# A three-layer graph convolution kernel: first edges gathered by an accumulating DMA, a new order in conv 2, and conv 1's bias written into PSUM by ScalarE

## What is computed

```python
def gcn_conv(x, W, b, src, dst, n):
    xw = x @ W
    s, d = concat([src, arange(n)]), concat([dst, arange(n)])
    deg = segment_sum(ones_like(d), d); dinv = rsqrt(deg)
    return segment_sum((dinv[s] * dinv[d])[:, None] * xw[s], d) + b

h = relu(layernorm(x))
a = gelu(layer_norm(gcn_conv(h, W1, b1), gamma1, beta1))          # conv 1
a = layer_norm(gcn_conv(a, W2, b2), gamma2, beta2)                # conv 2
x = x + gelu(a + h)
out = x + gcn_conv(relu(layernorm(x)), W3, b3)                    # conv 3
```

## Time and profile before

| what | value |
|---|---|
| median of 3 runs | 3601.41 us (3600.72 to 3601.57) |
| the profiled execution, its own time | 3601.81 us |
| its span, first to last instruction | 3599.8 us |
| busy over the span | PE 85%, DVE 87%, POOL 58%, ACT 46% |
| mean granted TensorE clock | 0.991 |
| data moved | 914.70 MB, 254 GB/s on average |

### The profile page before, as it was taken

One profiled execution on the slowest core, in us unless ns is written; L12 is line 12 of the kernel. 1 busy time (PEld: TensorE's weight loads), 2 busy tenths in 40 slices (PEclk: granted clock), 3 DMA queues, 4 the chain that ended last, 5 costly groups with the idle time before them and its releaser, 6 DMA issues. The chain is left out here.

```text
span 3599.8 us, 61879 instructions
## 1 busy us (share of the span) xinstructions
PE 3057.2 (85%) x16897; PEld 2498.2 (69%) x16897; DVE 3139.7 (87%) x6745; ACT 1650.5 (46%) x2375; POOL 2095.7 (58%) x1853
## 2 busy tenths in 40 slices
PE   8133299999999997999999999999488888888888
PEld 2022188888888886777777777778477777777777
DVE  9899789999999996888888888888688888888887
ACT  0366445555555553777777777777311111111111
POOL 0122256556556654677777777777466666666665
PEclk9999999999999998999999999999799999999999
DMA  3499967777777775888888888888477777777775
GB/s 118 163 408 418 365 215 221 220 225 222 218 223 223 220 219 171 289 295 299 297 296 295 296 298 295 297 295 288 162 241 246 241 246 242 241 246 238 246 240 190
DMA packets 277302, 914.70 MB, mean 254 GB/s; under 512 B 47617, under 2 KB 49511, under 8 KB 277246
## 3 DMA queue, kind: packets, MB, share of 16 engines
q1 hardware_dynamic: 191614, 683.15, 53.1%
q0 software_dynamic: 85632, 230.90, 22.9%
HBM read 653.47 MB, written 308.59 MB: 267 GB/s over the span
## 5 line engine op out<-in xcount | busy, mean ns | idle before, releaser
L840 POOL DMA_INDIRECT g<-H,idx x1062 | 1212.3, 1142 | 614.8 <-issue 428.9
L895 ACT ACTIVATE ahi<-agg 128x1024 fp32r<-128x1024 f32 x354 | 360.9, 1019 | 1039.1 <-PE agg L1171 1039.1
L1189 PE MATMUL out<-Whi,ahi 128*128 128x512 f32 x2832 | 768.9, 393 | 0.0
L1189 PE MATMUL out<-Wlo,ahi 128*128 128x512 f32 x2832 | 763.6, 391 | 0.0
L1189 PE MATMUL out<-Whi,alo 128*128 128x512 f32 x2832 | 761.2, 391 | 0.5 <-DVE alo L1006 0.5
L1162 PE MATMUL agg<-ident,self 128*128 128x128 f32 x2832 | 474.5, 279 | 220.9 <-DVE self L998 171.9
L1189 PEld LDWEIGHTS out<-Wlo,ahi 128*128 128x128 f32 x2832 | 531.6, 188 | 119.6
L1189 PEld LDWEIGHTS out<-Whi,alo 128*128 128x128 f32 x2832 | 531.6, 188 | 114.1 <-DVE alo L1006 1.0
L1189 PEld LDWEIGHTS out<-Whi,ahi 128*128 128x128 f32 x2832 | 510.4, 189 | 91.1
L1162 PEld LDWEIGHTS agg<-ident,self 128*128 128x128 f32 x2832 | 339.3, 142 | 315.8 <-DVE self L998 220.6
L1171 PE MATMUL agg<-sv,vhi 128*128 128x256 f32 x1416 | 384.0, 304 | 66.2 <-DVE sv L986 66.2
(11 more groups left out here) (175 smaller groups left out, 4137.5 us busy)
## 6 DMA issues: line engine op xcount, KB each, us to landing
self<-H SPq DMA_DIRECT2D x351, 512.0 KB, 5.1
H<-ho SPq DMA_DIRECT2D x250, 512.0 KB, 4.2
x<-in_x_dram SPq DMA_DIRECT2D x165, 512.0 KB, 6.2
X<-x SPq DMA_DIRECT2D x117, 512.0 KB, 4.3
x<-X SPq DMA_DIRECT2D x117, 512.0 KB, 7.2
out_dram<-conv SPq DMA_DIRECT2D x117, 512.0 KB, 6.3
H<-x SPq DMA_DIRECT2D x48, 512.0 KB, 9.6
g<-H,idx POOLq DMA_INDIRECT x1062, 4.3
```

Source lines behind the costliest of these rows:

```text
L840: pool.indirect_dma_start(g[:, c, :], None, H[q][0:end, :], bass.IndirectOffsetOnAxis(ap=own[:, c:c + 1], axis=0), bounds_check=end - 1, o ...
L895: nc.scalar.activation(Ahi[p.slot(2)][:, :], Agg[p.slot(2)][:, :], ACT.Copy)\
L1189: m = nc.tensor.matmul(o, a[u][:, c:c + P], w[q][:, f, :], start=(n == 0), stop=(third and n == 3 * KD - 1))
```

## The change

1. The accumulating gather. `SelfP` gets four buffers. The two first-edge gathers now name the own rows as their destination and carry `compute_op` add, so that the DMA adds the edge's row to what lies there; nodes without an edge have an index out of bounds and are skipped in all three convs. POOL therefore waits for `self_in` (own rows landed) ahead of the gathers. `add_first`, `has_first`, the padded zero rows of `H` and, in conv 2, the eight transposes of L1165 are gone.
2. Conv 1's bias. ACT writes bias times root of degree into the two PSUM banks of `Out` ahead of `multiply` (`seed`, an activation of 128x512 for each half), waits for `centre(p-2)` for that, and the first product adds to it. The two products of L1194 and the load of `root` go from conv 1. Conv 2 keeps both. Four products ahead of conv 1 touch the banks once.
3. Conv 2's order. On DVE, ACT and POOL the body is rewritten as below; `x2_var_eps`, `squares` and what follows lag one pair more. POOL's `residual(p)` waits for `x2_mean(p-2)` and stands ahead of `power` and the gathers.
4. The order of conv 1 and 3 on DVE. Conv 1: `over_low(p+2)`, `normal(p-1)`, `indices`, `stats(p)`, `low(p+1)`, `mean_var`, `var_eps`, `centre`. Conv 3: `over_low(p+2)`, `indices`, `low(p+1)`, `result(p)`.
5. `sv`, `x2_mean` and `x2_var_eps`, which were `tensor_scalar`, are now `scalar_tensor_tensor` with a tile of ones (or of EPS) as a second SBUF input.

```diff
@@ gather, POOL
                         if has(known, k - 2):
-                            if added:
-                                pool.wait_ge(sum_done.sem, sum_done.upto(p.after(-2)))
-                                pool.wait_ge(vlo_done.sem, vlo_done.upto(p.after(-2)))
-                            else:
-                                pool.wait_ge(agg_done.sem, agg_done.upto(p.after(-2)))
+                            pool.wait_ge(vlo_done.sem, vlo_done.upto(p.after(-2)))
                         pool.wait_ge(idx_made.sem, idx_made.upto(p))
+                        pool.wait_ge(self_in.of(p), self_in.upto(p))
...
+                        rows = [SelfP[p.slot(4)][:, 0, :], SelfP[p.slot(4)][:, 1, :], V[p.slot(2)][:, :]]
+                        for c, op in enumerate((ALU.add, ALU.add, ALU.bypass)):
+                            pool.indirect_dma_start(rows[c], None, H[q][0:N, :],
                                                     bass.IndirectOffsetOnAxis(ap=own[:, c:c + 1], axis=0),
+                                                    bounds_check=N - 1, oob_is_err=False, compute_op=op)\
@@ seed, ACT (conv 1 alone)
+                    def seed(known, p):
+                        for j in range(2):
+                            if known is None or known >= 2:
+                                act.wait_ge(cg_done.sem, cg_done.upto(p.after(-2), j + 1))
+                            nc.scalar.activation(Out[2 * p.slot(2) + j][:, :], bias_b[0][:, :], ACT.Copy,
+                                                 scale=sqrt_deg[:, bass.ds(p.n * 2 + j, 1)]).then_inc(seeded.sem, 1)
@@ over_low, DVE
-                        nc.vector.tensor_scalar(Sv[p.slot(2)][:, :], col[:, :], over_to[:, bass.ds(p.n, 1)],
-                                                None, ALU.is_equal).then_inc(sv_made.sem, 1)
+                        nc.vector.scalar_tensor_tensor(Sv[p.slot(2)][:, :], col[:, :], over_to[:, bass.ds(p.n, 1)],
+                                                       ones[:, :], ALU.is_equal, ALU.mult).then_inc(sv_made.sem, 1)
@@ body, POOL
+                        if second and has(known, 0):
+                            residual(known, p)
+                        if second and (has(known, 0) or has(known, -2)):
+                            power(p)
                         if has(known, 3):
                             gather(known, p.after(3), 3)
@@ body, ACT
+                        if second:
...
+                                squares(p.after(-2))
...
+                                over_high(p.after(2))
...
+                                relu_x(of(known, 1), p.after(1))
...
+                                high(p.after(2))
...
+                                relu_x2(of(known, -2), p.after(-2))
...
+                                gelu(p)
+                            return
@@ body, DVE
+                        if second:
+                            if has(known, 1):
+                                low(p.after(1))
+                            if has(known, 0):
+                                stats(p)
+                                mean_var(p)
+                            if has(known, -2):
+                                v = x2_var_eps(p.after(-2))
...
+                                var_eps(p)
+                                centre(p)
+                            if has(known, 2):
+                                over_low(p.after(2))
+                            if has(known, -2):
+                                x2_coefs(p.after(-2))
+                            if has(known, 0):
+                                normal(known, p)
+                            if has(known, 4):
+                                indices(p.after(4))
+                            if has(known, -1):
+                                x2_sum(of(known, -1), p.after(-1))
+                                x2_mean(p.after(-1))
+                            return
@@ multiply, PE
+                        if first:
+                            pe.wait_ge(seeded.sem, seeded.upto(p, j + 1))
...
-                                                     start=(n == 0), stop=(third and n == 3 * KD - 1))
+                                                     start=(n == 0 and not first), stop=(not second and n == 3 * KD - 1),
+                                                     skip_group_check=first)
...
-                        if not third:
+                        if second:
                             pe.wait_ge(root_in.of(p), root_in.upto(p))
```

More of the change, by code:

```diff
@@ L148, in gnn_kernel @@
         bias_b, gamma_b, beta_b = vecs[0:3], vecs[3:5], vecs[5:7]
-        SelfP = [sb(f"self{u}", [P, 2, D]) for u in range(2)]
-        G = [sb(f"g{u}", [P, 3, D]) for u in range(2)]
+        gathered = sb("gathered", [P, 10, D])
+        SelfP = [gathered[:, 2 * u:2 * u + 2, :] for u in range(4)]
+        V = [gathered[:, 8 + u, :] for u in range(2)]
         Sv = [sb(f"sv{u}", [P, 2 * P], F32R) for u in range(2)]
@@ L193, in gnn_kernel @@
         x_co = [sb(f"x_co{u}", [P, 3, 2 * GROUP]) for u in range(4)]
[L195 removed]
+        stage = [t[:, j, :] for t in SelfP[0:2] for j in range(2)]
         WK = [(q, k) for q in range(3) for k in range(KD)]
@@ L617, in _ @@
                     m.then_inc(place_used, 1)
+                pe.wait_ge(tables_read, 1)
+                pe.wait_ge(w_free, 1)
+                for o in Out:
+                    nc.tensor.matmul(o[:, :], Whi[0][:, 0, 0:P], Whi[0][:, 0, :], start=True, stop=True)
         def if_general(engine, program):
@@ L810, in body @@
                             load_x(known, p.after(2), 2)
-                        if has(known, 3):
-                            load_self(known, p.after(3), 3)
                         if has(known, -lag):
@@ L847, in residual @@
                         R, Xt = RP[p.slot(2)], XtP[p.slot(4)]
+                        if second and has(known, -2):
+                            pool.wait_ge(mean2_done.sem, mean2_done.upto(p.after(-2)))
                         for j in range(2):
@@ L928, in squares @@
                     def squares(p):
-                        m = small[p.after(1).slot(4)]
+                        m = small[p.after(2).slot(4)]
                         for j in range(2):
@@ L959, in body @@
                             over_high(p.after(2))
-                        if not third and has(known, -1):
+                        if first and has(known, 1):
+                            seed(of(known, 1), p.after(1))
+                        if first and has(known, -1):
                             gelu(p.after(-1))
-                        if first and has(known, -1):
                             scale(of(known, -1), p.after(-1))
-                        if second and has(known, -2):
-                            relu_x2(of(known, -2), p.after(-2))
-                        if second and has(known, 0):
-                            relu_x(known, p)
-                        if second and has(known, -1):
-                            squares(p.after(-1))
                     turn(act, body)
@@ L1118, in body @@
                             indices(p.after(4))
-                        if has(known, 2):
-                            over_low(p.after(2))
-                            if added:
-                                add_first(p.after(2))
-                        if has(known, 1):
-                            low(p.after(1))
-                        if second and has(known, -1):
-                            x2_sum(of(known, -1), p.after(-1))
                         if third:
+                            if has(known, 1):
+                                low(p.after(1))
                             if has(known, 0):
@@ L1132, in body @@
                             stats(p)
-                        if second and has(known, -1):
-                            x2_mean(p.after(-1))
+                        if has(known, 1):
+                            low(p.after(1))
                         if has(known, 0):
                             mean_var(p)
-                        if second and has(known, -1):
-                            v = x2_var_eps(p.after(-1))
-                            if not has(known, 0):
-                                v.then_inc(ve_done.sem, 1)
-                        if has(known, 0):
                             var_eps(p)
@@ L1216, in convolution @@
                 for flag in (ve_done, rstd_done):
-                    flag.close(NPAIR + second)
-                root_in.close()
+                    flag.close(NPAIR + 2 * second)
                 ho_out.close()
```

199 lines of the change are left out of this document (89 added, 110 removed).

## The result

The change makes the kernel slower: 3910.4 us (3909.1 to 3913.7) against 3601.5 us, ratio 1.0859, 95% interval 1.0841 to 1.0878. The forecast was 3728 us, the range 3570 to 3860: the direction is right, the size is 182 us short and outside the range.

A forecast was written before the change was run, and what follows sets the result against it. The prediction took DVE to set the pace in all three convs, with PE close behind. Its terms: 3601.8 - 63 - 146 + 180 + 146 + 12 (gathers' starts) - 3 (preparation) = 3728 us, range 3570 to 3860.

The forecast's parts named there:

- Conv 2, the order: Conv 2: a serial chain through DVE and PE makes each pair 11.00 us against 9.46, +180 us.
- none of DVE, ACT and POOL binds: Conv 2: DVE has 8.3 us of work, ACT about 8, POOL 8, in a pair of 11 us.
- Conv 2, the clock: Conv 2: PE's pause of some 2.9 us drops its clock in two pairs of three, 1.9 us lost each, +146 us.
- The upper bound, every pair: Conv 2: every pair restarts with 5.6 us at half speed, 2.6 us lost, +304 us, 3886 us in all; chance 0.11.
- The accumulating gather: POOL's gathers in all convs: accumulating was taken to cost no more than plain, priced at nothing.
- 0.35 us for each would still be hidden: POOL: 0.35 us more for each accumulating gather would not lengthen the loops.
- the rival: Conv 3: accumulating gathers make POOL bind, up to 3914 us, at half of that 3821; chance 0.10.
- Conv 1: Conv 1: PE binds at 7.41 us a pair instead of 7.95, two products and DVE's addition gone, -63 us.
- Conv 3: Conv 3: DVE loses `add_first`, PE's wait goes, 7.41 us a pair instead of 8.65, -146 us.
- the sum gets nothing for it: Conv 3: `sv` may stretch by up to 2.6 us beside POOL, costing nothing, as DVE has 6.2 us against PE's 7.41.
- `sv` in conv 3 still near 3 us: Conv 3, DVE: a sign expected if the forecast held, `sv` taking near 3 us.
- the full case of the gather: Conv 3: two accumulating gathers take twice as long, POOL binds at 9.0 us, +186 us; conv 1 and 2 unchanged.

The follow-up runs named there:

- experiment 1: The change, with PE running ten further 128x512 products ahead of each pair's transposes in conv 2, their output overwritten: 3732.1 us.
- experiment 2: The change, with DVE's `vlo` and `sv` of pair p+2 moved ahead of `stats(p)` in conv 2, POOL's order left alone: 4345.4 us.
- experiment 3: The change, with POOL issuing the overflow gather (V) ahead of the two accumulating ones: 3713.8 us.
- experiment 4: The change, with all three gathers plain, so first-edge rows replace the own rows instead of being added: 3765.2 us.
- experiment 7: Experiment 3's kernel, with conv 1 without ACT's seeds and PE's two bias products back: 3782.7 us.
- experiment 9: Experiment 5's kernel, with `sv`, `x2_mean` and `x2_var_eps` as `tensor_scalar` again: 3663.3 us.
- experiment 5: Experiment 3's kernel; in conv 2 `vlo` and `sv` go ahead of `stats(p)` on DVE, `gather(p+3)` ahead of `residual(p)` and `power(p)` on POOL: 3677.6 us.

## Why the prediction was right in direction and wrong in size

*Conv 2, the order* (+180): right. The chain measured 11.07 us, experiment 1 put its cost at 190 us, and the pause ended by DVE's `sv` is 3.01 us. The step that said none of DVE, ACT and POOL binds held in the change itself; experiment 2 shows that the slack of POOL's queue behind `power` was used up by the same order.

*Conv 2, the clock* (+146): right in kind, 24 us short. "Two pairs of three" was 82 of 117; a fall cost 2.1 us, not 1.9 (the sum took 1.25 us a pair for two thirds of 1.9, a little low), since between two pauses PE stood at the low level for 4.7 us on average (3.3 to 6.0) where it fell, not for 4.1. The upper bound, every pair, did not come: two pauses of 3.02 and 3.01 us in a row went either way. The Trainium skill, "TensorE: Matmul & The Clock Gate", section "HAM oscillation — how this bites in real kernels", tells of a kernel that waits some 3 to 5 us between bursts and starts every one slow; here, with pauses at the short end of that, 7 in 10 did. The price rested on a single pause of the trace before, so that it came this close is in part luck.

*The accumulating gather* (nothing): this step failed. "0.35 us for each would still be hidden" rested on a wrong picture of the cover. The term was 0.5 us each (1.55 us against 1.03, past the 1.4 us that the prediction itself named as a sign of being wrong), and it is paid in three ways, of which the prediction saw one. POOL's work in conv 3 is longer than the 7.41 us that the sum gave the pair: with V first it is full, as the rival said, at 7.66 us a pair, 7.76 in the round shown (experiment 3). V, third in the queue, lands late, and ACT, DVE and PE wait behind it in turn, in conv 1 too, for which the bound said "unchanged" (experiments 3 and 4). And the lateness moves `vlo` (41 pairs) or `sv` (11) to beside the residual, with the indices behind it. Together they are 145 us (experiment 4), against misses of 52 and 98; the share of each way is not measured.

*Conv 1* (-63): the terms were right and the period was not reached. With V in time it is 7.285 us, 0.12 below the sum, and the two products are worth 0.52 us a pair (experiment 7), not 0.46. The seeds cost nothing, as said.

*Conv 3* (-146): "the sum gets nothing for it" on the stretch of `sv` failed, and so did the sign "`sv` in conv 3 still near 3 us": its median is 0.48, and 11 of the 118 pairs have the 3 us. What is stretched instead is mostly `vlo`, by 108 us in all over conv 3, against 29 for `sv`. Such a stretch fits into DVE's idle time, but `indices` stand behind both, and POOL waited for those, 81 us in all behind a stretched `vlo` and 13 behind a stretched `sv`. A stall was costed by the engine's spare time and not by who waits for its queue. The new form of `sv` did not stay clear of POOL, as argued from the earlier trace rows; the earlier trace rows, and experiment 9 for a smaller instruction, show that the old form doesn't either.

*The range.* 3914 us, the full case of the gather, was within 4 us of the result, but by accident: it took 186 us from conv 3 alone, where the runs have 150 us of the gather's in conv 1 and 3 together and 34 of conv 2's.

## What to carry to other kernels

An order written by hand has a pair of slack here and there; before a producer is moved behind a wait, follow its consumers through every queue and close the loop with its landing time. Put first in a queue what the chain waits for, here V ahead of rows that are needed a pair later: 197 us from one line, some 135 of them in conv 1 and 3. And read an idle stretch for what runs under it: the wait that the new order removed was cover for an instruction that cannot run beside POOL's additions.

## What the runs showed of the hardware

- An indirect DMA of 128 rows that accumulates takes 1.55 us on POOL, a plain one 1.03, and a 2 KB row that is added takes 178 ns (median) on a DMA engine, against 159 ns for a plain packet of two rows.
- A DVE instruction of 2 elements with its data in SBUF takes 2.5 us beside POOL's additions of 2.5 to 3.1, as `tensor_scalar` and as `scalar_tensor_tensor`; the integer copy of 3 elements (`idx`) waits likewise, up to 3.2 us in the change's conv 3. BATCH_NORM_AGGREGATE took 0.25 us within the same addition (experiment 5). The Trainium skill, "SBUF — State Buffer", section "Who interferes with whom", names as open to this an instruction with two SBUF inputs and, in their two-port modes, `tensor_scalar` and copies; the traces agree for all three.
- Around pauses of PE of the same length, 3.02 and 3.01 us, TensorE's clock fell once and held once. Ten products of 128x512 put into such pauses kept it at 1.00 (experiment 1).
- DMA at a share of 0.98 and 288 GB/s did not slow a loop that PE bound at 7.28 us.
